# An attention and expert-network kernel: when weight loads, zero rows and half rows are loaded, and unread matmuls ahead of PE's waits in the output projection

## The reference

```
x = x + attention(layernorm(x)) @ proj_w.T + proj_b
f = layernorm(x)                       # second half, 4096 tokens
aff = f @ centroids.T; e = argmax(aff)
alpha = sigmoid(aff[e])
h = relu(layernorm(f, ln_g[e], ln_b[e]) @ w1[e].T + b1[e])     # 256 -> 1024
y = f + h @ w2[e].T + b2[e]                                    # 1024 -> 256
out = x + alpha * y + (1 - alpha) * f
```

## Time and profile before

| what | value |
|---|---|
| three executions | 884.49, 884.2, 879.96 us (median 884.2) |
| profiled execution: its own time | 886.25 us |
| profiled execution: span of the instructions | 884.5 us |
| mean granted TensorE clock | 0.967 of full |
| PE busy | 812.1 us (92%) |
| DVE, ACT, POOL busy | 599.5, 508.4, 340.6 us |
| HBM traffic | 139 GB/s over the span |

### The profile page before, as it was taken

The page is one execution under the profiler, slowest core; times in us unless marked ns, Lnnn a source line. Parts: engine busy times, 40 slices in busy tenths (PEclk is TensorE's granted clock), DMA queues, the critical chain, the costliest instruction groups (busy, mean ns, idle before and its releaser), DMA issues. The chain is left out here.

```text
span 884.5 us, 24359 instructions
## 1 busy us (share of the span) xinstructions
PE 812.1 (92%) x8788; PEld 497.3 (56%) x8789; DVE 599.5 (68%) x1161; ACT 508.4 (57%) x1175; POOL 340.6 (39%) x476
## 2 busy tenths in 40 slices
PE   7999859889979999999999988777999999999984
PEld 4555423333334444443344335456999999999853
DVE  5888999779969999999999605754733333333342
ACT  4767427668858888888888892023333333333331
POOL 9999653233333433334343332524111111133211
PEclk9999979999989999999999999988899999999998
DMA  7578532543453343433335115865555555555550
GB/s 281 179 231 255 170 119 69 175 169 53 111 106 91 95 100 97 90 87 86 86 81 159 51 42 180 277 189 196 173 186 182 180 180 183 187 187 189 179 173 4
DMA packets 63355, 128.90 MB, mean 146 GB/s; under 512 B 16982, under 2 KB 44247, under 8 KB 56983
## 3 DMA queue, kind: packets, MB, share of 16 engines
q1 hardware_dynamic: 59094, 112.53, 42.9%
q0 software_dynamic: 4160, 15.03, 4.6%
HBM read 99.89 MB, written 22.98 MB: 139 GB/s over the span
## 5 line engine op out<-in xcount | busy, mean ns | idle before, releaser
L917 ACT ACTIVATE arena<-ps_pair 128x512 f32<-128x512 f32 (+2 forms) x640 | 317.9, 556 | 76.6 <-PE ps_pair L1240 73.7
L997 DVE TENSOR_REDUCE B_block_max<-ps_item 128x8 f32<-128x1024 f32 x288 | 335.4, 1217 | 37.4 <-PE ps_item L1144 37.1
L1240 PE MATMUL ps_pair<-q_stack,k_stack 99*32 99x512 bf16 (+7 forms) x3072 | 198.5, 334 | 9.4 <-DMA q_stack<-B_nm 6.7
L831 POOL TENSOR_SCALAR_AFFINE_SELECT arena<-arena 128x256 f32<-128x256 f32 x256 | 102.4, 409 | 160.2 <-ACT arena L917 158.5
L1257 PE MATMUL ps_pair<-arena,B_v_quad 128*32 128x512 f32 (+3 forms) x1536 | 157.0, 493 | 0.9 <-ACT B_oacc L936 0.7
L1240 PEld LDWEIGHTS ps_pair<-q_stack,k_stack 99*32 99x32 bf16 (+1 forms) x3072 | 69.1, 96 | 130.0 <-ACT arena L917 62.1
L2037 PEld LDWEIGHTS C_bank<-arena 128*128 128x128 f32 x1024 | 122.5, 196 | 5.2 <-ACT arena L1558 3.7
L2037 PE MATMUL C_bank<-arena 128*128 128x128 f32 x1024 | 123.0, 280 | 2.0 <-ACT arena L1558 2.0
L1144 PE MATMUL ps_item<-k_stack,q_stack 64*128 64x128 bf16 (+2 forms) x1280 | 108.2, 267 | 15.9 <-DVE B_block_max L997 8.9
L2061 PE MATMUL C_ps_p<-arena 128*128 x512 | 117.4, 381 | 3.2 <-issue 3.1
L1588 ACT ACTIVATE arena<-C_bank,ffn_columns 128x128 f32<-128x128 f32 x128 | 36.6, 368 | 116.8 <-PE C_bank L2037 108.0
(11 more groups left out here) (204 smaller groups left out, 777.0 us busy)
## 6 DMA issues: line engine op xcount, KB each, us to landing
arena<-in_w_exp SPq DMA_DIRECT2D x41, 1024.0 KB
qk_parts<-arena SPq DMA_DIRECT2D x32, 384.0 KB, 3.4
q_stack<-qk_parts SPq DMA_DIRECT2D x96, 128.0 KB, 3.3
k_stack<-qk_parts SPq DMA_DIRECT2D x64, 128.0 KB, 3.4
arena<-in_w_exp POOLq DMA_DIRECT2D x6, 1024.0 KB, 7.1
rows<-payload SPq DMA_DIRECT2D x32, 130.5 KB
arena<-in_x SPq DMA_DIRECT2D x8, 512.0 KB, 4.7
arena<-in_x_feat SPq DMA_DIRECT2D x8, 512.0 KB, 5.7
```

The source lines that it names most:

```text
L831: pool.affine_select(out=block_p, in_=block_p, compare_op=ALU.is_ge, fill=0.0, base=0, pattern=[[0, 2], [1, P]], channel_multiplier=-1).th ...
L917: act.activation(pr[s % PR][:, h:h + 2 * n - 1:2, 0:W], ps_s[(EXPS * Q.const + exps_to[s] + u) % R][:, 0:n * W].rearrange("p (h n) -> p h ...
L997: dve.tensor_reduce(bmx[:, g:QH:GH, first:first + 3 * gap + 1:gap], src[:, :, :].rearrange("p c (b n) -> p c b n", n=P), AX.X, ALU.max).th ...
L1240: mm = pe.matmul(bank[at:at + 32, :], ks[rows, r, half, bass.ds(g * SEQ + kb * P + at, 32)], qs[rows, r, half, bass.ds(g * SEQ + c * QW + ...
```

## The change

Four edits. First, `early_at` becomes `(1, 2, 3, 4, 5, 14)` and the loads move from k == 2 to k == 4 (`W2_AT`): one 1 MB load in each of steps 1 to 5 and 14, four blocks into the step. Second, the nine zero rows move from n == 4, ahead of the stack loads, to n == 5, 7 and 9, three each, behind them. Third, half slots get buffers of their own (`half_rows`, one for each of the 7, with a semaphore each), loaded by SP at n = 24 to 30 behind `load_w1`; they no longer wait for the ring. Fourth, `keep_busy(w)`: ahead of the waits of pairs 2 to 14 PE issues two float32 matmuls of 256 columns of constants, six at w == 11, into PSUM banks that nobody reads at that time.

```diff
+        half_rows = ctx.enter_context(nc.sbuf_tensor("half_rows", [P, HALVES, P + PAYW - DIM], F32))
+        s_rh = [sem(f"half_rows_loaded{k}") for k in range(HALVES)]
         def load_rows(sp, S):
-            at = sp.value_load(slot_tab[0:1, 1, bass.ds(S.value(), 1)], min_val=0,
-                               max_val=DUMMY_ROW + (HT if is_half(S) else 0))
+            at = sp.value_load(slot_tab[0:1, 1, bass.ds(S.value(), 1)], min_val=0, max_val=DUMMY_ROW)
+            sp.dma_start(rows[:, S.ring(RD), :], pay_d[bass.ds(at, P), :]).then_inc(s_rl[S.ring(RD)], 16)
+
+        def load_half_rows(sp, k):
+            at = sp.value_load(slot_tab[0:1, 1, bass.ds(FULL + k, 1)], min_val=0, max_val=DUMMY_ROW + HT)
+            sp.dma_start(half_rows[:, k, 0:P],
+                         pay_d[bass.ds(at, HT), 0:DIM].rearrange("t (a n) -> a t n", a=DC)).then_inc(s_rh[k], 16)
+            sp.dma_start(half_rows[:, k, P:P + PAYW - DIM],
+                         pay_d[bass.ds(at, HT), DIM:PAYW].unsqueeze(0).to_broadcast([DC, HT, PAYW - DIM])).then_inc(s_rh[k], 16)
...
-        early_at = (1, 1, 2, 2, 14, 14)
+        early_at = (1, 2, 3, 4, 5, 14)
+        W2_AT = 4
...
-                    if n.const == 4:
-                        sp.wait_ge(s_pad0, 2)
-                        for e in range(NE + 1):
-                            sp.dma_start(pay_d[e * REGION:e * REGION + P, :], padrow).then_inc(s_pad, 16)
                     if n.const >= 3:
                         spread_inverse(sp, n.const - 3)
                     Q = n + 2
                     if Q.within(NQ):
                         load(Q)
+                    if n.const in (5, 7, 9):
+                        if n.const == 5:
+                            sp.wait_ge(s_pad0, 2)
+                        for e in range(3 * (n.const - 5) // 2, 3 * (n.const - 5) // 2 + 3):
+                            sp.dma_start(pay_d[e * REGION:e * REGION + P, :], padrow).then_inc(s_pad, 16)
...
-                        if k == NM_AT + 1:
+                        if k == W2_AT:
                             for e in [e for e in range(LOADED) if early_at[e] == i.const]:
                                 pool.dma_start(arena[:, e * W2C:(e + 1) * W2C], w_exp[e][:, W1C:WCOLS]).then_inc(s_w, 16)
...
                 def rows_of(S):
-                    if S.within(NSLOT):
+                    if S.within(NSLOT) and not is_half(S):
...
                         load_w1(sp, W)
+                    if n.reg is None and COPY_AT <= n.const < COPY_AT + HALVES:
+                        load_half_rows(sp, n.const - COPY_AT)
...
+                def keep_busy(w):
+
+                    if w < NP - 1:
+                        for i in range(6 if w == 2 * FIRST_GROUPS + 3 else 2):
+                            pe.matmul(bank[:, i % 2, 0:DIM], ident, cst[:, 0:DIM], start=True, stop=True)
+
                 for w in range(NP):
                     if w == 3 * KB // 2:
                         pe.wait_ge(s_nm, NQ // 2)
                     if w >= 2:
+                        keep_busy(w)
                         pe.wait_ge(s_x2, w - 1)
                         pe.wait_ge(s_lg, w - 1)
```

More of the change, by code:

```diff
@@ new lines, in row_data, with row_scalar, wait_rows @@
+        def row_data(S):
+            return half_rows[:, S.const - FULL, 0:P] if is_half(S) else rows[:, S.ring(RD), 0:DIM]
+        def row_scalar(S, c):
+            if is_half(S):
+                return half_rows[:, S.const - FULL, c - P:c - P + 1]
+            return rows[:, S.ring(RD), c:c + 1]
+        def wait_rows(eng, S):
+            if is_half(S):
+                eng.wait_ge(s_rh[S.const - FULL], 32)
+            else:
+                wait_dma(eng, s_rl, S)
+        phase_route_experts(nc, x, pay_d, load_w1, load_rows, load_half_rows, row_data, row_scalar, wait_rows, w2s, w1b, s_w1, cols, b2, cst, ident, eps, slot_tab, col, b2r,
@@ L1528, in normalize @@
                     if S.within(NSLOT):
-                        wait_rows(act, s_rl, S)
+                        wait_rows(act, S)
                         wait(act, s_tx, S, 1, -1)
                         wait(act, s_tl, S, 1, -1)
-                        row = rows[:, S.ring(RD), :]
                         n = P if is_half(S) else DIM
-                        act.activation(zz[:, S.ring(2), 0:n], row[:, 0:n], ACT.Identity, bias=row[:, COL_B:COL_B + 1],
-                                       scale=row[:, COL_S:COL_S + 1]).then_inc(s_zz, 1)
+                        act.activation(zz[:, S.ring(2), 0:n], row_data(S), ACT.Identity, bias=row_scalar(S, COL_B),
+                                       scale=row_scalar(S, COL_S)).then_inc(s_zz, 1)
                 for w in range(NP):
@@ L1604, in emit @@
                     if S.within(NSLOT):
-                        wait_rows(act, s_rl, S)
+                        wait_rows(act, S)
                         wait(act, s_res, S, 1, -1)
-                        act.activation(al[:, S.ring(2), 0:1], rows[:, S.ring(RD), COL_GATE:COL_GATE + 1], ACT.Exp,
+                        act.activation(al[:, S.ring(2), 0:1], row_scalar(S, COL_GATE), ACT.Exp,
                                        scale=-1.0).then_inc(s_ex, 1)
@@ L1833, in tail @@
                     if S.within(NSLOT):
-                        row = rows[:, S.ring(RD), :]
                         wait(dve, s_zz, S, 1, 1)
                         n = P if is_half(S) else DIM
-                        dve.scalar_tensor_tensor(out=row[:, 0:n], in0=zz[:, S.ring(2), 0:n], scalar=row[:, COL_K:COL_K + 1], in1=row[:, 0:n],
+                        dve.scalar_tensor_tensor(out=row_data(S), in0=zz[:, S.ring(2), 0:n], scalar=row_scalar(S, COL_K), in1=row_data(S),
                                                  op0=ALU.mult, op1=ALU.add).then_inc(s_tl, 1)
@@ L1870, in keep_ids @@
                 def keep_ids(S):
-                    at = rows[:, S.ring(RD), COL_ID:COL_ID + 1].bitcast(I32)
+                    at = row_scalar(S, COL_ID).bitcast(I32)
                     if is_half(S):
@@ L1924, in emit @@
                         dve.scalar_tensor_tensor(out=res[:, S.ring(2), 0:k], in0=y[:, S.ring(2), 0:k], scalar=al[:, S.ring(2), 2:3],
-                                                 in1=rows[:, S.ring(RD), 0:k],
+                                                 in1=row_data(S),
                                                  op0=ALU.mult, op1=ALU.add).then_inc(s_res, 1)
```

14 lines of the change are left out of this document (1 added, 13 removed).

## The result

| | median | all executions |
|---|---|---|
| before | 884.35 us | 884.49, 884.20, 879.96, 884.64 |
| after | 869.09 us | 868.69, 869.49, 867.85, 870.39 |

The ratio is 0.984, with a 95% interval of 0.981 to 0.987: the change wins 15.3 us. The forecast was 21.1 us less, 863.1, with 859 to 867 as the forecast's own range; 869.1 lies outside that and inside the whole range of 855 to 871. The profiled execution took 868.69 us, with a span of 866.9 against 884.5 before.

The account below looks back on a forecast made before the run. Attention was taken as running at PE's pace with a few holes, the projection and the end as waiting. -18.4 + 1.0 - 4.6 + 0.9 = -21.1 gave 863.1 us, own range 859 to 867, whole range 855 to 871.

Parts of the forecast that it names:

- Holes removed in attention: Attention: the four overlong steps, three with two weight loads and one with the zero rows, return to 23.90 us; -18.4 us.
- Loads against the stack: Attention steps 1 to 5: the moved weight load makes the stack loads late; +1.0 us for all five, between 0 and 8.
- Rival (a): Attention: stack loads late in each of steps 1 to 5 by the full collision; +7 us, 870; chance 0.15.
- rival (b): Attention: the collision grows, each of steps 1 to 5 loses 4.4 us; slower than before, 887; chance 0.02.
- The Trainium skill's rule: Attention: DMA engines take turns between queues by whole packets, so the load-against-stack cost would be some 0.5 instead of 1.0.
- The copy of the maxima: Attention: with the load at k == 4 the copy is well under way, one load behind it; its wait costs nothing.
- Half rows: From 836 us on: early-loaded half rows remove PE's waits for ACT, all but one relu wait; -4.6 us, bounds -3 and -5.7.
- Unread matmuls: Output projection: fillers delay pair 15 by 3.0 us but keep its clock up, winning 2.1; +0.9 us, bounds +3.9 and -3.
- Rival (c): Output projection: the fillers hold PE and the clock falls anyway; +3 us, 866; chance 0.14.
- Rival (d), the lull: 609 to 626 us, PE partly idle at low clock: lull goes, 855, chance 0.10; or grows, 871, chance 0.05.
- Rival (e): Attention: the holes are no DMA matter and only SP's order helps; -8 - 4.6, 872; chance 0.02.
- The forecast case: Whole kernel: all attention steps 23.9 us apart, pair 15 at 2.05 us, half slots 4.9 us apart; 863.1 us; chance 0.52.

Follow-up runs that it names:

- The kernel with even steps: The changed kernel with one weight load in each of steps 2, 4, 6, 8, 10 and 14; 883.9 us, 0.997 of the kernel before.

## Why the prediction was right or wrong

**The sum** was -21.1 and the medians gave -15.3, inside the range and 6.0 us above the forecast. The traces gave -17.6 between spans. The profiled execution of the kernel before lay 1.9 us above the median and that of the kernel after 0.4 below, which makes up the rest.

**Holes removed in attention, -18.4: right.** The stage gave -12.7, with losses of 5.9 in steps 3 and 5; without these it is -18.6. Putting the old weights back brought 4.43 and 4.07 us in steps 1 and 2 and 1.75 in step 14, where the forecast had 4.40, 4.47 and 1.46. The zero rows cost nothing behind the stack loads.

**Loads against the stack, +1.0: the step that failed.** This term of the sum measured 5.9. The 4.9 beyond the forecast are most of the 6.0 by which the median missed. The prediction reasoned that "the load has a start of one microsecond plus what the engines have idle" against 1.4 us that are free. The start was right, one microsecond in every step, and in steps 1, 2 and 4 the load cost nothing. Missed was what else is in flight, the spread first of all. In the kernel before it stands behind SP's copy too, 2.1 us ahead of the stack loads of step 3, but the prediction counts the bytes of the load and the stack alone:

```profile
211.85 1.60 SPq L733 DMA_DIRECT2D q_stack<-B_nm  x2
213.50 0.61 SPq L244 DMA_DIRECT2D arena<-inverse_sums  x1
215.64 0.60 SPq L377 DMA_DIRECT2D q_stack<-qk_parts  x1
```

The remark that "Steps 1 and 2 have fewer other DMAs" named the difference and gave it no price. Rival (a) had the right wait, and its 870 is close to the 869.1 measured, but not for its reason: it had a full collision of 1.6 us in each of five steps, and there were 3 us in each of two. That the loads lengthen these steps is shown; that the spread is the reason is read off the pattern and not shown. Where all three transfers met, up to 6.6 us were lost in a step, above the 3.0 that one matrix takes at the rate of the earlier trace rows and above the 4.4 a step of rival (b). The kernel with even steps came to within 0.3% of the one before in just this way.

The Trainium skill's rule (DMA: Bandwidth & Descriptors, Queues, rings and completion order), that each engine takes turns between queues, would have made it 0.5. The measurement decides: each of the bad steps lost several times that. No run tells whether the order between the queues or the engines' own pace is the reason.

**The copy of the maxima, nothing: right, and more widely than argued.** I took it that the load had to come after the copy. With one load a step it may stand ahead of it: at k == 2 the copy was issued 0.1 to 2.9 us after the load and PE did not wait.

**Half rows, -4.6: right,** -5.0 in the stage, and 4.62 us a slot instead of the forecast's 4.9.

**Unread matmuls, +0.9: near in sum, wrong in its parts.** The stage gave -1.5, not +0.9, and the stretch behind it +0.5. Kernels with and without them on one chip differ by 0.2 to 0.5 us from the first pair to the first half slot on two chips. On the third those with them are 2.9 to 8.0 us longer and differ by 5.1 among themselves, which settles nothing. That the sum came out near nothing is luck, for two errors offset each other. Right was that the clock held with them: 2.05 us for pair 15 in every kernel that has them, against 3.89, 3.62 and 2.92 in the three without (the Trainium skill, TensorE: Matmul & The Clock Gate, Part 1, What's actually happening, says the same of work and idle time). Right was also that the transposes come late, by 2.9 instead of 3.9. Wrong was the register reading: I took 0.9 of 2.22 us back, and all of it went, so that pair 15 started 0.35 us late and not 3.0. But then the first slots wait for ACT (3.74 us here, 0.81 in the kernel with loads at k == 2), and what was won is gone. Rival (c), the clock falling anyway, is out.

**Rival (d), the lull:** it neither went nor grew; the stretch that holds it took 0.5 us more. **Rival (e),** no DMA matter, is out by the kernel with the old weights, in which steps 1, 2 and 14 are long again.

The chances were sound in sign. The forecast case itself, every step at 23.9, did not happen; it is what the load at k == 2 then gave (0.977 and 0.974, the forecast's being 0.976).

## What to carry to other kernels

When a background load is moved, write down every transfer that is in flight at the new place, on all queues, with the time each is issued in the steps where its queue runs late, and not only the one it is moved away from: here the load just ahead of the stack loads was free in some steps and cost 2 to 7 us in those where the spread stood within 2.5 us ahead of it, or where it met the end of the stack loads. Give several steps the same edit and compare the steps within one trace; the one that differs says more than the sum does. Matmuls that nobody reads held the clock here, and the time in front of pair 15 went with them, but it won nothing in the whole, since PE then waited for ACT.

## What the runs showed of the hardware

**The difference between chips lies mostly in one stretch.** The kernel before had medians of 874.3 and 873.4 us on two chips and 886.7 and 886.4 on two others. The profiled kernels differ there in the stretch from the end of pair 15 to the first half slot: 228.9 to 230.3 us on the first two, 239.3 to 242.6 on the other two, with the same instructions there. (Each chip was used at one time only, so chip and time can't be told apart.) Most of it is in the first 45 us, as two windows show, of the load at k == 2 on one of the first two chips and of the changed kernel on one of the others:

```profile
571.60:616.60 45.00, 44.19 (x329) 41.89 (x327) 29.75 (x124) 18.70 (x57) 18.93 (x20) 1.00 0.74 239
```

```profile
580.00:625.00 45.00, 38.80 (x243) 35.67 (x242) 24.31 (x105) 14.78 (x45) 16.78 (x18) 0.85 0.58 189
```

This is the lull of the earlier trace rows. In the profile after it looks like this, first PE, then ACT:

```profile
600.69 0.38 PE L2080 MATMUL C_ps_p<-arena 128*128 x1 [0.93 <-issue]
602.12 0.86 PE L2080 MATMUL C_ps_p<-arena 128*128 x2 [1.05 <-issue]
604.25 5.03 PE L2080 MATMUL C_ps_p<-arena 128*128 x10 [1.27 <-issue]
```

```profile
606.52 1.14 ACT L1601 ACTIVATE arena<-C_bank,ffn_columns 128x128 f32<-128x128 f32 x4 [13.64 <-remote]
```

PE gets its matmuls one by one, with a microsecond between them, and ACT does nothing for 13.6 us with no releaser named. On the first two chips PE misses at most 1.4 us of those 45. The stretch is 9 to 14 us longer on the others, most of the difference between the chips and more than half of what this change wins. What causes it stays open.

**A 1 MB load and a small copy.** With two loads issued ahead of it the copy of the maxima reached PE 9.5 us after its issue; with one load ahead PE did not wait for it at all. By an estimate from the 344 GB/s of the earlier trace rows, two loads take 6.1 us, so their bytes alone don't account for the 9.5.
